# VectorE's multiply and scan of a state-space stage, split by state into two of each, a PSUM bank each

## What is computed

```python
u = jax.nn.silu(conv(u)); delta = jax.nn.softplus(dt @ dtw + dtb); A = -jnp.exp(A_log)
def step(h, inp):
    d_t, b_t, c_t, u_t = inp
    dA = jnp.exp(d_t[..., None] * A)
    h = dA * h + (d_t * u_t)[..., None] * b_t[:, None, :]
    y = jnp.einsum('bdn,bn->bd', h, c_t)
    return (h, y)
y = (scan of step over the 512 steps) + u * Dp
y = (y * jax.nn.silu(z)) @ ow            # then a layer norm of y + x
```

## Time and profile before

| | us |
|---|---|
| median of 3 runs | 3717.27 |
| their range | 3712.19 to 3720.76 |
| profiled execution, its span | 3722.3 |
| state-space loop in it, about | 1366 to 3306 |
| VectorE busy over the span | 2837.2 |
| TensorE (matmul) busy | 2986.0 |
| GpSimd busy | 2058.8 |
| ScalarE busy | 1877.4 |

### The profile page before, as it was taken

The page is one execution under the profiler, slowest core; times in us unless marked ns, Lnnn a source line. Parts: engine busy times, 40 slices in busy tenths (PEclk is TensorE's granted clock), DMA queues, the critical chain, the costliest instruction groups (busy, mean ns, idle before and its releaser), DMA issues. The chain is left out here.

```text
span 3722.3 us, 48432 instructions
## 1 busy us (share of the span) xinstructions
PE 2986.0 (80%) x18383; PEld 1641.8 (44%) x18386; DVE 2837.2 (76%) x3771; ACT 1877.4 (50%) x2961; POOL 2058.8 (55%) x1053
## 2 busy tenths in 40 slices
PE   8969999556499378998899889988989889658733
PEld 3438888533377223344344434344434444234412
DVE  3566676656211339999999999999999999987688
ACT  2433333124111057666776777667776777424334
POOL 0024545212300317798988988898889898952100
PEclk8877787778699778999999999999999999988856
DMA  1000000000333233434344344434444444430000
GB/s 49 0 1 4 4 4 4 7 20 0 124 123 123 52 108 136 156 137 163 136 146 151 132 171 137 144 136 151 155 144 146 144 132 144 146 107 10 3 19 23
DMA packets 120561, 343.54 MB, mean 92 GB/s; under 512 B 14875, under 2 KB 45554, under 8 KB 119570
## 3 DMA queue, kind: packets, MB, share of 16 engines
q1 hardware_dynamic: 114450, 331.91, 26.2%
q0 software_dynamic: 3072, 6.00, 0.8%
q10 hardware_dynamic: 2816, 2.62, 0.2%
HBM read 328.21 MB, written 14.68 MB: 92 GB/s over the span
## 5 line engine op out<-in xcount | busy, mean ns | idle before, releaser
L2020 POOL TENSOR_TENSOR mb_h<-mb_h,mb_BC 128x1024 f32<-128x1024 f32 x512 | 1211.1, 2385 | 325.7 <-DVE mb_h L2285 325.5
L2285 DVE TENSOR_TENSOR_SCAN mb_h<-mb_dA,mb_bx 128x1024 f32<-128x1024 f32 x512 | 1170.4, 2286 | 50.9 <-ACT mb_dA L2145 33.6
L2384 PE MATMUL mb_y<-mb_h,ident 128*128 128x512 f32 x2048 | 972.5, 619 | 141.6 <-POOL mb_h L2020 141.1
L2145 ACT ACTIVATE mb_dA<-mb_delta,mb_A 128x511 f32<-128x511 f32 x1024 | 657.6, 712 | 216.7 <-DVE mb_h L2285 212.1
L2384 PEld LDWEIGHTS mb_y<-mb_h,ident 128*128 128x128 f32 x2048 | 390.4, 196 | 688.1 <-issue 442.8
L2281 DVE TENSOR_TENSOR mb_bx<-mb_du,mb_BC 128x1024 f32<-128x1024 f32 x512 | 630.6, 1232 | 46.7 <-DMA mb_BC<-mamba_BC 5.6
L250 PE MATMUL mb_p<-mb_xT,mb_in_w 128*128 128x512 f32 x512 | 271.5, 680 | 85.5 <-ACT mb_sz L2064 79.5
L250 PE MATMUL mb_p<-mb_upad,mb_convd 128*128 128x512 f32 x512 | 225.0, 592 | 0.8 <-ACT mb_upad L2052 0.8
L250 PEld LDWEIGHTS mb_p<-mb_xT,mb_in_w 128*128 128x128 f32 x512 | 110.2, 219 | 238.5 <-issue 137.8
L1738 DVE TENSOR_TENSOR me_h<-me_s,me_p 128x320 f32<-128x320 f32 x64 | 31.2, 487 | 220.9 <-ACT me_s L1715 220.9
L1692 POOL DMA_INDIRECT me_y<-expert_results,slot x32 | 31.1, 972 | 258.2 <-DMA expert_results<-me_oe 248.7
(11 more groups left out here) (440 smaller groups left out, 5502.7 us busy)
## 6 DMA issues: line engine op xcount, KB each, us to landing
mb_BC<-mamba_BC SPq DMA_DIRECT2D x256, 1024.0 KB, 5.2
me_W<-in_L_ffn_W SPq DMA_DIRECT2D x24, 1024.0 KB, 9.3
mb_in_w<-in_L_attn_in_proj_w SPq DMA_DIRECT2D x4, 1024.0 KB, 5.0
mb_convd<-in_mamba_taps SPq DMA_DIRECT2D x4, 1024.0 KB, 7.1
expert_rows<-me_zero SPq DMA_DIRECT2D x1, 2560.0 KB, 10.0
x<-in_x SPq DMA_DIRECT2D x4, 512.0 KB, 6.1
me_xe<-expert_rows SPq DMA_DIRECT2D x8, 256.0 KB, 10.6
expert_results<-me_oe ACTq DMA_DIRECT2D x8, 256.0 KB, 7.6
```

Source lines behind the costliest of these rows:

```text
L2020: tt(hk, hk, buffer(k, it)[:, 1, :, :], ALU.mult).then_inc(*pos(f"hc{k}{part}"))
L2145: i = av(dA[k % 2][:, c, s, 1:], delta[:, it % 2, mc, 1:], ACT.Exp, scale=A[:, MC * layer(it) + mc, n:n + 1])
L2285: nc.vector.tensor_tensor_scan(flat(h[k % NBUF][:, c, :, :]), flat(dA[k % 2][:, c, :, :]), flat(full(bx)), 0.0, ALU.mult, ALU.add).then_in ...
L2384: i = mm(ybank[c][:, :], m.ident[:, :], h[k % NBUF][:, c, s, :], start=False, stop=e == HALF - 1 and s == SU - 1)
```

## The change

On VectorE `bx` becomes two tiles of one PSUM bank each, one for each state of the pair. The multiply becomes two of 512, the scan two of 512, in the order multiply 0, multiply 1, scan 0, scan 1. Each multiply waits for the scan that read its own bank in the half before (`sc0`, `sc1`), each scan for its own multiply; the wait for `dA` stands before scan 0. The counter now has four steps a half. GpSimd and ScalarE wait for the second scan (`sc1`), and ScalarE's copy of `du` for the second multiply (`bx1`). The other engines' instructions stay as they were. The diff, without the lines that only rename `dA`, `hc` and `sc` to the new spelling:

```diff
--- before.py
+++ after.py
@@ -1838,7 +1838,7 @@
         ybank = [pb(f"mb_y{i}", [P, 512]) for i in range(CU)]
         du = [pb(f"mb_du{i}", [P, 512]) for i in range(CU)]
-        bx = pb("mb_bx", [P, SU, T])
+        bx = [pb(f"mb_bx{i}", [P, T]) for i in range(SU)]
         bank = [pb(f"mb_p{i}", [P, 512]) for i in range(2)]
@@ -1847,13 +1847,13 @@
-        per = lambda *names: " ".join(f"{n}{k}{c}" for k in us for c in "ab" for n in names)
+        per = lambda *names: " ".join(f"{n}_{k}{c}" for k in us for c in "ab" for n in names)
...
-        dvf, dvs = signal("vector_f", "zs"), signal("vector_s", per("bx", "sc"))
+        dvf, dvs = signal("vector_f", "zs"), signal("vector_s", per("bx0", "bx1", "sc0", "sc1"))
@@ -2015,9 +2015,9 @@
                         for c, part in enumerate("ab"):
-                            po.wait_ge(*dvs.at(f"sc{k}{part}", it))
+                            po.wait_ge(*dvs.at(f"sc1_{k}{part}", it))
                             hk = h[k % NBUF][:, c, :, :]
-                            tt(hk, hk, buffer(k, it)[:, 1, :, :], ALU.mult).then_inc(*pos(f"hc{k}{part}"))
+                            tt(hk, hk, buffer(k, it)[:, 1, :, :], ALU.mult).then_inc(*pos(f"hc_{k}{part}"))
@@ -2097,7 +2097,7 @@
                     for c, part in enumerate("ab"):
-                        a.wait_ge(*dvs.at(f"bx{kb}{part}", tb))
+                        a.wait_ge(*dvs.at(f"bx1_{kb}{part}", tb))
@@ -2139,11 +2139,11 @@
                         for c, part in enumerate("ab"):
-                            a.wait_ge(*dvs.at(f"sc{kb}{part}", tb))
+                            a.wait_ge(*dvs.at(f"sc1_{kb}{part}", tb))
...
@@ -2187,7 +2187,6 @@
-                flat = lambda t: t.rearrange("p s t -> p (s t)")
@@ -2277,13 +2276,14 @@
                             kp, tp = (k, it) if c else before(k, it, 1)
                             if k % HALF == 0:
                                 v.wait_ge(*acd.at(f"du{half}{part}", it))
-                            v.wait_ge(*dvs.at(f"sc{kp}{'ab'[1 - c]}", tp))
-                            tt(full(bx), du[c][:, :].rearrange("p (o t) -> p o t", o=1).broadcast_to([P, SU, T]),
-                               buffer(k, it)[:, 0, :, :], ALU.mult).then_inc(*dvs(f"bx{k}{part}"))
-                            v.wait_ge(*dvs.at(f"bx{k}{part}", it))
-                            v.wait_ge(*acs.at(f"dA{k}{part}", it))
-                            nc.vector.tensor_tensor_scan(flat(h[k % NBUF][:, c, :, :]), flat(dA[k % 2][:, c, :, :]), flat(full(bx)), 0.0,
-                                                         ALU.mult, ALU.add).then_inc(*dvs(f"sc{k}{part}"))
+                            for s in range(SU):
+                                v.wait_ge(*dvs.at(f"sc{s}_{kp}{'ab'[1 - c]}", tp))
+                                tt(bx[s][:, :], du[c][:, :], buffer(k, it)[:, 0, s, :], ALU.mult).then_inc(*dvs(f"bx{s}_{k}{part}"))
+                            v.wait_ge(*acs.at(f"dA_{k}{part}", it))
+                            for s in range(SU):
+                                v.wait_ge(*dvs.at(f"bx{s}_{k}{part}", it))
+                                nc.vector.tensor_tensor_scan(h[k % NBUF][:, c, s, :], dA[k % 2][:, c, s, :], bx[s][:, :], 0.0,
+                                                             ALU.mult, ALU.add).then_inc(*dvs(f"sc{s}_{k}{part}"))
```

More of the change, by code:

```diff
@@ L1934, in _ @@
                         kb, tb = before(k, it, NBC)
-                        sp.wait_ge(*pos.at(f"hc{kb}b", tb))
+                        sp.wait_ge(*pos.at(f"hc_{kb}b", tb))
                         load_bc(k, it)
@@ L2072, in softplus1 @@
                     if cs[0] == 0:
-                        a.wait_ge(*acs.at(f"dA{UN - 1}b", j - 2))
+                        a.wait_ge(*acs.at(f"dA_{UN - 1}b", j - 2))
                         a.wait_ge(*pof.at("du", j - 2))
@@ L2145, in _ @@
                                 i = av(dA[k % 2][:, c, s, 1:], delta[:, it % 2, mc, 1:], ACT.Exp, scale=A[:, MC * layer(it) + mc, n:n + 1])
-                            i.then_inc(*acs(f"dA{k}{part}"))
+                            i.then_inc(*acs(f"dA_{k}{part}"))
                         if k % HALF == 0:
@@ L2381, in _ @@
                         for c, part in enumerate("ab"):
-                            t.wait_ge(*pos.at(f"hc{k}{part}", it))
+                            t.wait_ge(*pos.at(f"hc_{k}{part}", it))
                             for s in range(SU):
```

## The result

The kernel after takes 3704.88 us (median of 14 runs, 3695.26 to 3711.07), the one before 3714.18 us (14 runs beside them): ratio 0.9969, 95% interval 0.9960 to 0.9979. By the ratio it is 11.5 us faster, with an interval of 7.8 to 14.9 us; the two medians are 9.3 apart. (One execution of run 10, further down, ran in a slower state, 5223 us at granted clock 0.557, and is left out of its times and ratio.) The forecast was 5.0 us, "within 0.2%", and it gave a gain of more than that a chance of 0.25. The time lies in the range, near its lower end; the forecast of no measurable change was wrong.

A forecast was written before the change was run, and what follows sets the result against it. GpSimd, TensorE and ScalarE stretches bound the stage, with VectorE on the path under 6 us in 121. Gains 0.2 (beats) + 2.5 + 2.3 (end) = 5.0 us off 3717.3 gave 3712 us, range 3703 to 3740.

The forecast's parts named there:

- What bounds the kernel: State-space stage: GpSimd 43 us, TensorE 58, ScalarE 11 set the pace; VectorE counts only for unit 10, under 6 in 121.
- the beat: State-space stage: time between starts of unit 10's half-a scan in successive turns, 121.2 us, expected to stay so.
- That half waits go: VectorE: no instruction waits for its direct neighbour, so the next starts 0.08 us before the record ahead ends, not 0.04 after.
- Rivals 2 and 3: VectorE: no overlap behind a multiply writing PSUM, 3740 us, chance 0.09; no overlap anywhere, 3858 us, chance 0.05.
- rival 3: VectorE: no overlap anywhere, by the skill's rule; a part costs 3.98 us, the kernel 3858 us; chance 0.05.
- five rows against rival 3: Trace rows cited as showing VectorE instructions that start before the record ahead ends, about 0.08 us early.
- The size of a part: VectorE's multiplies and scans for one half of a unit: 3.506 us instead of 3.638, 0.13 less.
- The beats: 14 turn-to-turn distances of the stage: unit 10's stretch goes from 5.87 to 5.86 us, gain 0.01 x 14 = 0.2.
- The end: After the last waiting unit 10 scan: 19 parts give 2.5 us, units 4 to 6 nothing, the last 18 parts 2.3.
- The start: Before the first waiting scan of unit 10, half a: no gain, since it waited for ScalarE too.
- Where the idle time would show: VectorE: 5 to 6 us idle before unit 10's scan instead of 2, longer waits for B and C at unit 7.
- The chances: Whole kernel: faster 0.25, slower 0.15, within 0.2% (7.4 us) 0.60; the forecast itself had 0.79.

The follow-up runs named there:

- run 10: Kernel before, unsplit, with GpSimd's last two preparation operations cut to a quarter of their width and its layer norm in three pieces: 3691.3 us, ratio 0.9948.
- Runs 2 and 3: Kernel after plus unread 1024-wide VectorE products: behind half a of units 4 and 6, ratio 0.9979 to the kernel before; behind half a of unit 10 alone, 1.0003.
- run 1: Kernel after with the order multiply 0, scan 0, multiply 1, scan 1: 3764.2 us, ratio 1.0135 to the kernel before.
- run 4: Kernel before with the split in the last two of 16 turns alone, wide instructions raising VectorE's counter by 2: ratio 1.0051 to the kernel before.

## Why the forecast was right and where it failed

- **What bounds the kernel: right.** Each piece of the beat was where the prediction put it. From the records, before and after: scan 10a to the end of 10b 5.87 and 5.75 us, GpSimd's stretch 43.07 and 43.08, from there to the D term 3.21 and 3.21, TensorE up to the copy of y 58.07 and 58.07, ScalarE up to dA 10.79 and 10.79; the starts behind scan 10b and behind dA add 0.08 and 0.08, 0.10 and 0.03. Runs 2 and 3 show it by intervention.
- **That half waits go: right.** No neighbour waits for its neighbour, and the overlap is there behind an instruction that writes PSUM too, the case that no row had shown. Rivals 2 and 3 are out: run 1 has as many instructions as the kernel after and costs about 60 us more. The sentence of the Trainium skill that rival 3 rests on ("VectorE: DVE Perf Modes", section "The DRAIN you can't avoid": the flush behind an instruction can't be skipped by leaving out semaphores) does not hold for this sequence, whose instructions start 0.08 to 0.09 us before the record ahead ends. The same section does say that a next instruction which is not held starts earlier; the prediction had left that out. (It also counted five rows against rival 3; the two pairs of neighbours in the earlier trace rows are what speaks against it.)
- **The size of a part: this is the step that failed.** I took 0.70 - 0.08 for a multiply and 1.22 - 0.08 for a scan, and called 3.506 the lower bound. Measured, from start to start, are 0.59 and 1.12: the fixed time of an instruction, beyond its 512 elements (0.533 = 1.232 - 0.699 and 1.067 = 2.286 - 1.219), is 0.04 to 0.06 us, not 0.07 to 0.09. Two things were missing. The overlap behind a multiply is 0.093, and a record that starts in the shadow of the one ahead is itself shorter: 676 and 690 ns for a multiply (medians), not 699, and 1.20 for a scan, not 1.22. The trace of before had a sign of this: the four bn_stats of 256 at the earlier trace rows start 0.32 to 0.33 us apart, of which 0.27 are elements, by the rate of the multiply. The gain of a part is 0.22 us (3.638 - 3.417), not 0.13.
- **The beats.** Expected 0.01 each, measured 0.20. 0.12 is the stretch of unit 10, 5.87 us before and 5.75 after (forecast 5.86), with the smaller fixed times. 0.07 the forecast did not have at all: scan 10a starts 0.03 us after the record of its dA ends, not 0.10. It carries two waits, and only one rides on the instruction itself; the other is an instruction of the sequencer ahead of it. Before, the wait for dA was the separate one, after it is that for the multiply; the trace has the separate one as a record of its own, at 2417.91 before and, for the multiply, at 2407.52 after. Run 1 shows the price of this: its scan 0, whose wait for the multiply is separate, starts 0.10 behind it, its scan 1 0.03. 14 x 0.20 = 2.7 us.
- **The end.** Expected 4.8 us, measured 6.4. The division was right. From multiply 7a to the end 18 parts bring 3.8 us (expected 2.3), all from the size of a part. From the end of 3b to 7a nothing, as expected: the load holds the multiply, which had no idle time before and has 1.51 now:

```profile
3227.43 1.30 DVE L2281 TENSOR_TENSOR mb_bx<-mb_du,mb_BC 128x512 f32<-128x512 f32 x2 [1.51 <-DMA mb_BC<-mamba_BC]
```

  Up to the end of 3b the parts bring 2.7 of 19 x 0.22 = 4.2, because the load for unit 1 hangs on GpSimd in its full stretch as well, which I had not seen; multiply 1a waits for it:

```profile
3184.74 1.30 DVE L2281 TENSOR_TENSOR mb_bx<-mb_du,mb_BC 128x512 f32<-128x512 f32 x2 [1.10 <-DMA mb_BC<-mamba_BC]
```

- **The start.** Expected 0, measured 0.9. That scan 10a waits in turn 0 does not mean that the scans ahead of it are off the path: in the first units of turn 0 TensorE still waits for the products that follow the scans. In the kernel before:

```profile
1389.30 1.98 PE L2384 MATMUL mb_y<-mb_h,ident 128*128 128x512 f32 x4 [1.52 <-POOL mb_h L2020]
```

  The size of this gain is less sure than the other two. Five profiles of split kernels with the same code up to there have 78.7 to 80.4 us for the stretch, four unsplit ones 80.8 to 81.0. The cause was read from the trace and not tried by a run.
- **Where the idle time would show: wrong for scan 10a.** I expected 5 to 6 us before it, and about 85 us for the line's wait for dA; measured are 1.0 and 20.5. The clip behind unit 9 waits for ScalarE too, so that part of it stands there (44 us more than before, 3 a turn), and 1.2 us of each turn are filled by the clip, which takes 2.45 us now. The longer waits for B and C at unit 7 came, and others at unit 1.
- **What the misses add up to.** The loop gained 10.0 us where 5.0 were forecast: 2.5 more in the beats (about 1.5 from the size of a part, 1.0 from the place of the wait), 1.6 more at the end and 0.9 at the start.
- **The chances.** With 0.22 a part the prediction's own sum gives 14 x 0.12 + 19 x 0.22 + 18 x 0.22 = 9.8 us, 0.26%, on the other side of the 0.2% line. A forecast so near to a line should have carried the error of its main term, 0.13, as a chance; I had called its low end excluded. That the time still lies in the range is in part luck: of the 7 us between 3712 and 3704.88, 3 are the kernel before, whose median came out at 3714.18 and not 3717.27, and the lower edge, 3703, had been set for noise and not for this.

## What to carry to other kernels

Find the beat first, then ask what an engine contributes to it: VectorE was busy 95% of the time and stood on the path for 6 us in 121. When the saved time goes into waits, as 7 us a turn did here, look for the place where the engine that sets the pace waits for the faster one and move work into it: the split brought 0.3%, the split and the new order on GpSimd 0.8%, and the new order alone nothing that could be measured. And put dependent instructions of one engine two places apart: this order is worth 0.34 us a part against the same instructions in pairs. Not tried were the wide instructions in such an order (multiply a, multiply b, scan a, scan b), with two `bx` of two banks.

## What the runs showed of the hardware

- VectorE's fixed time for an instruction with no wait on its neighbour was 0.04 to 0.06 us (from start to start, multiply 0.582 and 0.597 with 0.533 of elements, scan 1.110 and 1.127 with 1.067); with one, 0.17 (multiply and the gap behind it in run 1, 0.71).
- Raising a semaphore by 2 instead of 1 cost 0.055 to 0.07 us behind an instruction that the next one waits for (run 4: gaps of 0.09 and 0.105, against 0.035; gaps of 0.134, where the sequencer has a separate wait to do, stayed).
- A VectorE product with both sources in SBUF waited through up to three back-to-back GpSimd instructions: 8.96 us, where it took 2.29 with GpSimd idle. The clip, 2048 wide in SBUF, took 1.20 us mostly and 2.47 us when it started in the middle of a GpSimd product.
